# One tile of sources for each block of 128 slots, and four sums in PSUM instead of two pairs of two

## The chip, the cores and the metric

The kernel runs on one core of a Trainium2 chip. The metric is the device time of one execution, in microseconds (us), from the start to the end of the program; a lower time is better. A core has five engines that run their own queues of instructions: TensorE (PE, with its weight loads as PEld), VectorE (DVE), ScalarE (ACT), GpSimd (POOL) and SyncE (SP). Each engine has a sequencer that reads its queue in order, does the register and semaphore instructions itself and hands the others to the engine; the profile marks what the sequencer does with a q (DVEq, PEldq).

## The reference

Four layers are added in turn to `x`, 2500 nodes by 256 features. The change touches the third, a graph attention with two heads of 128 features over 40000 edges, and the sort of the edges that it needs:

```python
def _gat_head(node_feats, W, a, src, dst, N):
    h = node_feats @ W
    a_l, a_r = (a[0, :C], a[0, C:])
    s_l = h @ a_l
    s_r = h @ a_r
    logits = s_l[src] + s_r[dst]
    e = jnp.exp(-jax.nn.leaky_relu(logits, negative_slope=ALPHA))
    row_sum = jax.ops.segment_sum(e, src, num_segments=N)
    h_prime = jax.ops.segment_sum(e[:, None] * h[dst], src, num_segments=N)
    return jax.nn.elu(h_prime / row_sum[:, None])
...
x = x + _L0_gnn_ref(_layernorm(x, axis=-1), edge_attr_256, src, dst, ...)
x = x + _L0_ffn_ref(_layernorm(x, axis=-1)[None], ...)[0]
x = x + _L1_gnn_ref(_layernorm(x, axis=-1), ..., edge_index, 2500)
x = x + _L1_ffn_ref(_layernorm(x, axis=-1)[None], ...)[0]
```

The first layer is a message passing over the same edges, the second a mixture of 16 experts with the best two of each node, the fourth an attention over 64 slices.

## The kernel before, in words

**Tiles of nodes.** The 2500 nodes stand as 125 lanes by 20 tiles; node n is in lane n // 20 of tile n % 20 (`LANES`, `TILES`).

**The sort.** So that a block of edges adds into one tile of sources, the edges are sorted by the tile of their source. Each tile's edges get a run of slots; the run is padded to a multiple of `unit` slots. Before, `unit` is `PAIR` = 256, so two blocks of 128 slots always share a tile, and the buffers have `PAIR_BLOCKS` = 352 blocks. With these inputs the 20 tiles have 1923 to 2083 edges each. Padded to 256 they fill 326 blocks, the last 26 of the 352 hold no edge at all; padded to 128 they would fill 323. The counting runs during the first layer (`count_bucket`), the numbering of the slots (`BucketSort.number`, L274 to L314) on VectorE at the start of `node_mlp`, before that stage's own work, and the last three instructions of it (L310, L313, L314) find for each pair of blocks its tile: a comparison of every pair's number with the 20 tile ends, on one lane, then a sum. Its result is `tile_row`. The placing of edges into slots (`Placing`, L354 to L381) is spread over the 54 blocks of the mixture of experts: for each of 320 columns of edges VectorE and ScalarE make one-hot rows and TensorE multiplies them twice into a table of 352 columns (L380).

**The attention over edges** (`attend_edges`, L1711 to L1898) works in groups of four blocks (`GROUP` = 4), 88 groups. For a group g

- GpSimd issues four indirect DMAs (L1769), each of which gathers 128 rows of 258 floats (the features and right scores of the edges' other ends) from `head_table` in DRAM into `got`. There are four buffers (`RB` = 4), and GpSimd waits only for the indices, which VectorE copies for group g + 4 in its iteration g (L1836).
- VectorE makes the one-hots of the sources' lanes (L1840), TensorE turns them (L1783), ScalarE copies them out of PSUM (L1820) and widens the others to f32 (L1823), and TensorE multiplies them with the tile's left scores (L1789). VectorE sums the three parts (L1846), adds the right scores once the gather has landed (L1850), applies the leaky relu (L1852), ScalarE the exponential (L1825), and VectorE multiplies the gathered rows by it (L1857, L1860).
- TensorE multiplies one-hots and weighted rows (L1799), two blocks into each of the two sums of `s_ps[u]`; two sets of two sums take turns, and a set is free once the sums of group g - 2 are added.
- VectorE adds each sum to its tile of the accumulator in SBUF (L1868). Which tile it is, it has to read: `tiles_of` (L1738) loads one register from `tile_row` for each sum, and TensorE's queue does the same for the left scores.

The order on VectorE is written out by hand. Iteration g is: one-hots of g + 1, weighting of g (L1857, L1860), indices of g + 4, `tiles_of` and the additions of g - 1, then L1846, L1850 and L1852 of g + 1. On TensorE it is `source_scores(g + 1)` and then `scatter(g)`. Four groups are one turn of a hardware loop.

```python
def accumulate(g, u, first=False):
    tiles = tiles_of(dve, g)
    dve.wait_ge(scattered, g + 1)
    for n, tile in enumerate(tiles):
        if not first or n > 0:
            dve.wait_ge(added, g * UN + n)
        dve.tensor_tensor(acc[:, tile, :], s_ps[u][0:LANES, n, 0:ROW], acc[:, tile, :], ALU.add).then_inc(added, 1)
```

Of the kernel before, what the change touches and what calls it, by code (L numbers as in the profile page):

```python
# [16 lines left out]
P = 128  # L17
# [11 lines left out]

PAIR = 2 * P  # L30
PAIR_BLOCKS = -(-((N_EDGES + TILES * (PAIR - 1)) // PAIR * 2) // (2 * GROUP)) * 2 * GROUP
MOE_BLOCKS = -(-((N_NODES * TOP + EXPERTS * (P - 1)) // P) // 6) * 6
# [78 lines left out]
class Shared:  # L111


    def __init__(self, nc, sb, sem):
# [12 lines left out]
        self.ones = sb("ones", [P, P])  # L127
        self.count_i = sb("count_i", [P, PAIR_BLOCKS], I32)
        self.count = sb("count", [P, PAIR_BLOCKS])
        self.count16 = sb("count16", [P, PAIR_BLOCKS], F16)  # L130
        self.ident16 = sb("ident16", [P, P], BF16)
# [28 lines left out]
def constants(nc, m, io):  # L160

    made = m.constants_made
    with nc.Block() as block:
# [16 lines left out]
        def _(pool):  # L180
# [13 lines left out]
            chain.link(pool.memset(m.ones[:], 1.0))  # L194
            chain.link(pool.iota(m.count_i[:], pattern=[[1, PAIR_BLOCKS]], base=0, channel_multiplier=0))
            chain.link(pool.iota(m.lane_i[:], pattern=[[0, 1]], base=0, channel_multiplier=1))
# [12 lines left out]
class BucketSort:  # L209
# [64 lines left out]
    def number(self, dve):  # L274
# [13 lines left out]
        if self.by_bucket:  # L288
# [8 lines left out]
            chain.link(nc.vector.tensor_tensor(slot[:], slot[:], self.part[:], ALU.add))  # L297
            self.past = seen[0:1].rearrange("p b c -> p (b c)")[:, 0:units * buckets].rearrange("p (u b) -> p u b", b=buckets)
        else:
# [9 lines left out]

        chain.link(nc.vector.tensor_tensor(  # L310
            self.past, m.count[0:1, 0:units].unsqueeze(2).to_broadcast([1, units, buckets]),
            last[0:1, :].unsqueeze(1).to_broadcast([1, units, buckets]), ALU.is_ge))
        chain.link(nc.vector.tensor_reduce(self.tile_f[:], self.past, AX_X, ALU.add))  # L313
        chain.link(nc.vector.tensor_scalar(out.tile_row, self.tile_f[:], float(buckets - 1), None, ALU.min))  # L314
# [1396 lines left out]
def attend_edges(nc, sem, m, r, sl, acc):  # L1711
# [19 lines left out]
    G = GROUP  # L1731
    UN = G * P // PAIR
    groups = PAIR_BLOCKS // G
    turns = groups // RB
# [5 lines left out]
    with ExitStack() as ctx:  # L1740
# [17 lines left out]
        sl_ps = ps("sl_ps", [P, 512])  # L1758
        s_ps = [ps(f"s_ps{u}", [P, UN, 512]) for u in range(2)]
        with nc.Block() as block:  # L1760
# [16 lines left out]
            def _(pe):  # L1777
# [15 lines left out]
                def scatter(g, u, wait_added=True):  # L1793
                    pe.wait_ge(hot_ready, g + 1)
                    pe.wait_ge(scaled, g + 1)
                    if wait_added:
                        pe.wait_ge(added, (g - 1) * UN)
                    for j in range(G):
                        last = nc.tensor.matmul(s_ps[u][0:LANES, j * UN // G, 0:ROW], hot[u][:, j, :], w[u][:, j, :],  # L1799
                                                start=j % (G // UN) == 0, stop=j % (G // UN) == G // UN - 1)  # L1800
                    last.then_inc(scattered, 1)

                source_scores(0, 0)
                for v in range(RB):
                    source_scores(v + 1, (v + 1) % 2)
                    scatter(v, v % 2, v >= 2)
                with pe.Fori(1, turns - 1) as i:
# [8 lines left out]
            @block.scalar  # L1816
            def _(act):
                def one_group(g, u, begun=True):
                    act.wait_ge(turned, g + 1)
                    nc.scalar.activation(hot_t[u][:], t_ps[0:LANES, :, :], ACT.Copy).then_inc(turned_in, 1)  # L1820
                    if begun:
                        act.wait_ge(scattered, g - 1)
                    nc.scalar.activation(hot[u][:], hot16[u][:], ACT.Copy).then_inc(hot_ready, 1)  # L1823
                    act.wait_ge(lrelu_ready, g + 1)
                    nc.scalar.activation(e[u][:], lrelu[u][:], ACT.Exp, scale=-1.0).then_inc(e_ready, 1)  # L1825

                for v in range(RB):
                    one_group(v, v % 2, v >= 2)
                with act.Fori(1, turns) as i:
                    for v in range(RB):  # L1830
                        one_group(RB * i + v, v % 2)

            @block.vector
            def _(dve):
# [27 lines left out]
                def accumulate(g, u, first=False):  # L1862
                    tiles = tiles_of(dve, g)
                    dve.wait_ge(scattered, g + 1)
                    for n, tile in enumerate(tiles):
                        if not first or n > 0:
                            dve.wait_ge(added, g * UN + n)
                        dve.tensor_tensor(acc[:, tile, :], s_ps[u][0:LANES, n, 0:ROW], acc[:, tile, :], ALU.add).then_inc(added, 1)  # L1868

# [578 lines left out]
def gnn_moe_gat_slice_kernel(nc, io_gine, io_moe, io_gat, io_slice, out):  # L2448

    with ExitStack() as ctx:  # L2450
# [3 lines left out]
        def sem(n):  # L2454
            return ctx.enter_context(nc.semaphore(n))

        m = Shared(nc, sb, sem)
        by_src = Ends(sb("slots_by_src_other", [P, PAIR_BLOCKS], I32)[:], sb("slots_by_src_lane", [P, PAIR_BLOCKS])[:],
                      sb("slots_by_src_tile_row", [1, PAIR_BLOCKS // 2], I32)[:])
        constants(nc, m, io_gine)  # L2460
        with ExitStack() as sorting:
            s = EdgeSort(nc, sorting, "by_src", by_src, PAIR_BLOCKS, PAIR)
            gather_and_update(nc, m, io_gine, s)
# [40 lines left out]
```

## Time and profile before

| | |
|---|---|
| three runs | 2787.79, 2793.99 (median), 2800.44 us |
| the profiled execution | 2793.28 us, its span 2791.5 us |
| mean granted clock of TensorE | 0.857 of full speed |
| busy share of the span | PE 75%, PEld 65%, DVE 59%, ACT 36%, POOL 51% |
| L1769, gathers of the attention | 352, 404.5 us busy, 1149 ns each in the mean |
| L1799, TensorE's sums | 704, 276.8 us busy, 561 ns each in the mean |

The profiled execution took 0.7 us less than the median of the runs. The span runs from its first to its last instruction. Times in the rows are us from the start of the span; those of one instruction are its start and its duration. "Idle before" names what ended the time in which the engine had nothing to run; "issue" is time for which the profile shows no wait.

### The profile page before, as it was taken

How to read it: one execution, taken by the hardware profiler on the slowest of the kernel's cores; microseconds unless marked ns; L12 is line 12 of the kernel's file. 1: busy time of each engine (PE TensorE's matmuls, PEld its weight loads, DVE VectorE, ACT ScalarE, POOL GpSimd, SP SyncE). 2: the span in 40 equal slices, each digit the busy share in tenths (PEclk: the TensorE clock that was granted, in tenths of full speed). 3: DMA queues.
4: the chain of work that ended last, by engine and by line, in shares of the span. 5: the costliest groups of instructions: out<-in, count | busy, mean ns of one | idle time of the engine just before them, and what ended most of it. 6: DMA issues, size and time to landing. Idle time of an engine off the chain costs nothing. (4 is left out here: it accounts for less than half of the span.)

```text
span 2791.5 us, 46568 instructions
## 1 busy us (share of the span) xinstructions
PE 2090.2 (75%) x13095; PEld 1806.7 (65%) x13096; DVE 1650.7 (59%) x4813; ACT 1008.1 (36%) x1931; POOL 1409.8 (51%) x1131
## 2 busy tenths in 40 slices
PE   3599989999999999919349999951366766662966
PEld 2588878888888888819338888851344444441855
DVE  5477776766666666666264444444555555556962
ACT  1244444544544444414115555530122222221311
POOL 1487787877877777720001111125377777770000
PEclk9799999999999999969569999985677667675978
DMA  6566666666666666550037677742233333361000
GB/s 166 137 122 132 128 126 131 133 132 129 133 130 132 131 132 128 113 115 1 38 106 236 237 240 245 245 139 57 70 90 89 90 88 92 90 86 31 1 9 37
DMA packets 186354, 325.62 MB, mean 117 GB/s; under 512 B 30014, under 2 KB 111723, under 8 KB 185298
## 3 DMA queue, kind: packets, MB, share of 16 engines
q0 software_dynamic: 85280, 141.65, 25.5%
q1 hardware_dynamic: 100118, 181.83, 21.0%
q10 hardware_dynamic: 900, 1.50, 0.2%
q8 instruction: 24, 0.39, 0.1%
q14 instruction: 32, 0.26, 0.0%
HBM read 260.52 MB, written 64.30 MB: 116 GB/s over the span
## 5 line engine op out<-in xcount | busy, mean ns | idle before, releaser
L631 POOL DMA_INDIRECT edge_sums<-edge_agg,edge_slot x316 | 553.9, 1753 | 174.8 <-issue 78.0
L1769 POOL DMA_INDIRECT att_got<-head_table,att_idx x352 | 404.5, 1149 | 143.7 <-issue 107.0
L622 POOL DMA_INDIRECT edge_nf<-node_table,edge_node_idx x316 | 325.7, 1031 | 152.4 <-issue 88.1
L750 ACT ACTIVATE edge_whole<-edge_h_ps,edge_b 128x512 f32<-128x512 f32 x316 | 216.5, 685 | 480.5 <-PE edge_h_ps L467 477.0
L465 PE MATMUL edge_e_ps<-edge_w_high,edge_hid_low 128*128 128x256 f32 x1264 | 356.7, 282 | 0.1
L466 PE MATMUL edge_e_ps<-edge_w_low,edge_hid_high 128*128 128x256 f32 x1264 | 355.8, 282 | 0.0
L467 PE MATMUL edge_e_ps<-edge_w_high,edge_hid_high 128*128 128x256 f32 x1264 | 355.4, 281 | 0.0
L1799 PE MATMUL att_s_ps<-att_w,att_hot 128*125 128x258 f32 x704 | 276.8, 561 | 4.6 <-issue 3.5
L465 PE MATMUL edge_h_ps<-edge_eat_high,edge_w_low 128*128 128x512 f32 x632 | 248.9, 394 | 23.6 <-DVE edge_eat_low L810 23.6
L1361 POOL DMA_INDIRECT moe_rows<-node_table,moe_idx x54 | 51.7, 958 | 398.4 <-DVE moe_idx L1472 398.1
L467 PE MATMUL edge_h_ps<-edge_eat_high,edge_w_high 128*128 128x512 f32 x632 | 252.3, 399 | 0.0
L819 DVE TENSOR_TENSOR edge_hid_low<-edge_whole,edge_hid_high 128x512 fp32r<-128x512 f32 x316 | 218.9, 693 | 54.3 <-ACT edge_hid_high L755 48.6
L466 PE MATMUL edge_h_ps<-edge_eat_low,edge_w_high 128*128 128x512 f32 x632 | 249.7, 395 | 0.0
L824 DVE TENSOR_TENSOR edge_pre<-edge_e_ps,edge_nf 128x1024 f32<-128x1024 f32 x79 | 96.8, 1225 | 257.6 <-DMA edge_nf<-node_table,edge_node_idx 205.2
L465 PEld LDWEIGHTS edge_e_ps<-edge_w_high,edge_hid_low 128*128 128x128 f32 x1264 | 244.6, 194 | 0.3 <-DVE edge_hid_low L819 0.3
L466 PEld LDWEIGHTS edge_e_ps<-edge_w_low,edge_hid_high 128*128 128x128 f32 x1264 | 244.3, 193 | 0.0
L467 PEld LDWEIGHTS edge_e_ps<-edge_w_high,edge_hid_high 128*128 128x128 f32 x1264 | 243.8, 193 | 0.0
L1799 PEld LDWEIGHTS att_s_ps<-att_w,att_hot 128*125 128x125 f32 x704 | 185.1, 276 | 47.2 <-issue 4.4
L1411 PE MATMUL moe_h_ps<-moe_xt,moe_w 128*128 128x128 f32 x1728 | 206.2, 278 | 10.7 <-DMA moe_w<-in_L_ffn_w_dram 8.9
L1411 PEld LDWEIGHTS moe_h_ps<-moe_xt,moe_w 128*128 128x128 f32 x1728 | 199.1, 193 | 17.2 <-issue 8.5
L1783 PEld LDWEIGHTS att_t_ps<-ident,att_hot 128*125 128x125 bf16 x352 | 38.0, 177 | 185.2 <-DVE att_hot L1840 180.3
L1783 PE MATMUL att_t_ps<-ident,att_hot 128*125 128x128 bf16 x352 | 48.2, 275 | 139.6 <-DVE att_hot L1840 139.1
(344 smaller groups left out, 4526.5 us busy)
## 6 DMA issues: line engine op xcount, KB each, us to landing
moe_w<-in_L_ffn_w_dram SPq DMA_DIRECT2D x162, 512.0 KB, 4.7
edge_ea<-in_edge_attr_dram SPq DMA_DIRECT2D x77, 448.0 KB, 5.1
edge_dst_row<-dst_rows SPq DMA_DIRECT2D x79, 256.0 KB, 4.5
routed<-moe_out SPq DMA_DIRECT2D x54, 128.0 KB, 6.2
att_got<-head_table,att_idx POOLq DMA_INDIRECT x352, 2.8
edge_nf<-node_table,edge_node_idx POOLq DMA_INDIRECT x316
edge_sums<-edge_agg,edge_slot POOLq DMA_INDIRECT x316
edge_ea<-in_edge_attr_dram SPq DMA_DIRECT2D x77, 64.0 KB, 5.4
```

The source lines that it names most:

```text
L465: pe.matmul(out, ll, rh, start=start, stop=False)
L466: pe.matmul(out, lh, rl, start=False, stop=False)
L467: return pe.matmul(out, lh, rh, start=False, stop=stop)
L622: pool.indirect_dma_start(nf[u][:, j, :], None, m.node_table[:, :], bass.IndirectOffsetOnAxis(ap=node_idx[u][:, j:j + 1], axis=0)).then_in ...
L631: pool.indirect_dma_start(m.sums[k][:, :], bass.IndirectOffsetOnAxis(ap=slot[u][:, j:j + 1], axis=0), agg[u][:, j, :], None, compute_op=AL ...
L750: act.activation(whole[c][:], h_ps[:, c % 2, 0:N], ACT.Relu, bias=b1[:, c:c + 1]).then_inc(hid_whole, 1)
L819: nc.vector.tensor_tensor(hidl[:, c, :], whole[c][:], hidh[:, c, :].bitcast(F32), ALU.subtract).then_inc(hid_ready, 1)
L824: nc.vector.tensor_tensor(pre[:], e_ps[:], nf[u][:], ALU.add).then_inc(summed, 1)
L1411: last = nc.tensor.matmul(h_ps[:, c, :], w[:, kd, c * P:(c + 1) * P], xt[u][:, kd, :], start=kd == 0, stop=kd == KD - 1)
L1769: pool.indirect_dma_start(got[v][:, j, :], None, m.head_table[:, :], bass.IndirectOffsetOnAxis(ap=idx[v][:, j:j + 1], axis=0)).then_inc(la ...
L1783: last = nc.tensor.transpose(t_ps[0:LANES, j, :], hot16[u][:, j, :], m.ident16[:])
L1799: last = nc.tensor.matmul(s_ps[u][0:LANES, j * UN // G, 0:ROW], hot[u][:, j, :], w[u][:, j, :], start=j % (G // UN) == 0, stop=j % (G // U ...
```

## The change

The unit of the sort becomes 128 slots, so each block has a tile of its own; `SRC_BLOCKS` is 336, in 84 groups. `tile_row` has 336 entries instead of 176. The comparison for it no longer fits its buffer at once and is done in two halves of 168 by 20. `s_ps` is one set of four sums: block j of every group has sum j, TensorE waits before each matmul for the addition of sum j of the group before, and VectorE waits before each addition for its own matmul. `UN`, the number of sums and of register loads in a group, goes from 2 to 4. A matmul no longer adds to the one before it in PSUM.

```diff
--- before.py
+++ after.py
@@ -27,8 +27,7 @@
 GROUP = 4
 
 
-PAIR = 2 * P
-PAIR_BLOCKS = -(-((N_EDGES + TILES * (PAIR - 1)) // PAIR * 2) // (2 * GROUP)) * 2 * GROUP
+SRC_BLOCKS = -(-((N_EDGES + TILES * (P - 1)) // P) // (4 * GROUP)) * 4 * GROUP
 MOE_BLOCKS = -(-((N_NODES * TOP + EXPERTS * (P - 1)) // P) // 6) * 6
 NODE_MID = N_NODES // 2
 SUMS = 2
...
@@ -295,7 +294,7 @@
                 chain.link(last_slots)
                 chain.link(nc.vector.tensor_reduce(to[:], self.numbers[:].rearrange("p b c -> p c b"), AX_X, ALU.add))
             chain.link(nc.vector.tensor_tensor(slot[:], slot[:], self.part[:], ALU.add))
-            self.past = seen[0:1].rearrange("p b c -> p (b c)")[:, 0:units * buckets].rearrange("p (u b) -> p u b", b=buckets)
+            self.past = seen[0:1].rearrange("p b c -> p (b c)")[:, 0:units // 2 * buckets].rearrange("p (u b) -> p u b", b=buckets)
         else:
             for b in range(buckets):
                 last_slots = nc.vector.scalar_tensor_tensor(seen[:, b, :], seen[:, b, :], off[:, b:b + 1], mask[:, b, :], ALU.add, ALU.mult)
@@ -307,10 +306,12 @@
         chain.link(nc.vector.tensor_scalar(slot_i[:], slot_i[:], P - 1, None, ALU.bitwise_and))
         chain.link(nc.vector.tensor_copy(out.pos, slot_i[:]))
 
-        chain.link(nc.vector.tensor_tensor(
-            self.past, m.count[0:1, 0:units].unsqueeze(2).to_broadcast([1, units, buckets]),
-            last[0:1, :].unsqueeze(1).to_broadcast([1, units, buckets]), ALU.is_ge))
-        chain.link(nc.vector.tensor_reduce(self.tile_f[:], self.past, AX_X, ALU.add))
+        some = self.past.shape[1]
+        for a in range(0, units, some):
+            chain.link(nc.vector.tensor_tensor(
+                self.past, m.count[0:1, a:a + some].unsqueeze(2).to_broadcast([1, some, buckets]),
+                last[0:1, :].unsqueeze(1).to_broadcast([1, some, buckets]), ALU.is_ge))
+            chain.link(nc.vector.tensor_reduce(self.tile_f[:, a:a + some], self.past, AX_X, ALU.add))
         chain.link(nc.vector.tensor_scalar(out.tile_row, self.tile_f[:], float(buckets - 1), None, ALU.min))
 
 
@@ -1729,8 +1730,8 @@
     scattered = sem("att_scattered")
     added = sem("att_added")
     G = GROUP
-    UN = G * P // PAIR
-    groups = PAIR_BLOCKS // G
+    UN = G
+    groups = SRC_BLOCKS // G
     turns = groups // RB
     assert groups % RB == 0
 
@@ -1756,7 +1757,7 @@
         w = sb("w", [P, G, ROW])
         t_ps = ctx.enter_context(nc.psum_tensor("att_t_ps", [P, G, P], BF16))
         sl_ps = ps("sl_ps", [P, 512])
-        s_ps = [ps(f"s_ps{u}", [P, UN, 512]) for u in range(2)]
+        s_ps = ps("s_ps", [P, UN, 512])
         with nc.Block() as block:
 
             @block.gpsimd
@@ -1793,17 +1794,15 @@
                 def scatter(g, u, wait_added=True):
                     pe.wait_ge(hot_ready, g + 1)
                     pe.wait_ge(scaled, g + 1)
-                    if wait_added:
-                        pe.wait_ge(added, (g - 1) * UN)
                     for j in range(G):
-                        last = nc.tensor.matmul(s_ps[u][0:LANES, j * UN // G, 0:ROW], hot[u][:, j, :], w[u][:, j, :],
-                                                start=j % (G // UN) == 0, stop=j % (G // UN) == G // UN - 1)
-                    last.then_inc(scattered, 1)
+                        if wait_added:
+                            pe.wait_ge(added, g * UN + (j - UN + 1))
+                        nc.tensor.matmul(s_ps[0:LANES, j, 0:ROW], hot[u][:, j, :], w[u][:, j, :], start=True, stop=True).then_inc(scattered, 1)
 
                 source_scores(0, 0)
                 for v in range(RB):
                     source_scores(v + 1, (v + 1) % 2)
-                    scatter(v, v % 2, v >= 2)
+                    scatter(v, v % 2, v >= 1)
                 with pe.Fori(1, turns - 1) as i:
                     for v in range(RB):
                         source_scores(RB * i + (v + 1), (v + 1) % 2)
@@ -1819,7 +1818,7 @@
                     act.wait_ge(turned, g + 1)
                     nc.scalar.activation(hot_t[u][:], t_ps[0:LANES, :, :], ACT.Copy).then_inc(turned_in, 1)
                     if begun:
-                        act.wait_ge(scattered, g - 1)
+                        act.wait_ge(scattered, (g - 1) * UN)
                     nc.scalar.activation(hot[u][:], hot16[u][:], ACT.Copy).then_inc(hot_ready, 1)
                     act.wait_ge(lrelu_ready, g + 1)
                     nc.scalar.activation(e[u][:], lrelu[u][:], ACT.Exp, scale=-1.0).then_inc(e_ready, 1)
@@ -1861,11 +1860,11 @@
 
                 def accumulate(g, u, first=False):
                     tiles = tiles_of(dve, g)
-                    dve.wait_ge(scattered, g + 1)
                     for n, tile in enumerate(tiles):
+                        dve.wait_ge(scattered, g * UN + (n + 1))
                         if not first or n > 0:
                             dve.wait_ge(added, g * UN + n)
-                        dve.tensor_tensor(acc[:, tile, :], s_ps[u][0:LANES, n, 0:ROW], acc[:, tile, :], ALU.add).then_inc(added, 1)
+                        dve.tensor_tensor(acc[:, tile, :], s_ps[0:LANES, n, 0:ROW], acc[:, tile, :], ALU.add).then_inc(added, 1)
 
                 def one_group(g, v, first=False, start=False):
                     u = v % 2
@@ -2455,11 +2454,11 @@
             return ctx.enter_context(nc.semaphore(n))
 
         m = Shared(nc, sb, sem)
-        by_src = Ends(sb("slots_by_src_other", [P, PAIR_BLOCKS], I32)[:], sb("slots_by_src_lane", [P, PAIR_BLOCKS])[:],
-                      sb("slots_by_src_tile_row", [1, PAIR_BLOCKS // 2], I32)[:])
+        by_src = Ends(sb("slots_by_src_other", [P, SRC_BLOCKS], I32)[:], sb("slots_by_src_lane", [P, SRC_BLOCKS])[:],
+                      sb("slots_by_src_tile_row", [1, SRC_BLOCKS], I32)[:])
         constants(nc, m, io_gine)
         with ExitStack() as sorting:
-            s = EdgeSort(nc, sorting, "by_src", by_src, PAIR_BLOCKS, PAIR)
+            s = EdgeSort(nc, sorting, "by_src", by_src, SRC_BLOCKS, P)
             gather_and_update(nc, m, io_gine, s)
             mixture(nc, sem, m, io_moe, s)
         graph_attention(nc, sem, m, io_gat, by_src)
```

## Rows read from the trace of the kernel before

**Rows 1.** The page: busy tenths of 40 slices of the span

```profile
POOL 1487787877877777720001111125377777770000
```

**Rows 2.** Waits from 2006 to 2528 us: us in total, times, longest

```profile
DVE att_z L1850 <- DMA att_got<-head_table,att_idx: 183.6, 85, 3.8
...
POOL att_got L1769 <- issue: 105.5, 346, 0.3
```

**Rows 3.** Timeline of GpSimd in the middle of the attention: start us, us

```profile
2204.98 2.14 POOL L1769 DMA_INDIRECT att_got<-head_table,att_idx  x1 [0.30 <-issue]
2207.42 0.95 POOL L1769 DMA_INDIRECT att_got<-head_table,att_idx  x1 [0.30 <-issue]
```

**Rows 4.** Timeline of VectorE, one group between two landings: start us, us

```profile
2204.08 0.17 DVE L1850 TENSOR_TENSOR att_z<-att_parts,att_got 128x8 f32<-128x8 f32 x1 [2.45 <-DMA att_got<-head_table,att_idx]
...
2205.06 1.22 DVE L1857 TENSOR_TENSOR att_w<-att_got,att_e 128x1024 f32<-128x1024 f32 x1
...
2206.65 1.00 DVE L1868 TENSOR_TENSOR gat_acc<-att_s_ps,gat_acc 125x258 f32 x2 [0.21 <-issue]
...
2207.56 0.17 DVE L1846 TENSOR_REDUCE att_parts<-att_sl_ps 128x8 f32<-128x24 f32 x1
...
2210.33 0.17 DVE L1850 TENSOR_TENSOR att_z<-att_parts,att_got 128x8 f32<-128x8 f32 x1 [2.60 <-DMA att_got<-head_table,att_idx]
...
2212.89 0.43 DVE L1868 TENSOR_TENSOR gat_acc<-att_s_ps,gat_acc 125x258 f32 x1 [0.22 <-issue]
```

**Rows 5.** Instructions of L1738, 2205.0 to 2206.6 us: duration ns min/median/max, first and last start

```profile
L1738 DVEq TENSOR_LOAD <-slots_by_src_tile_row x2: 300/301/302, 2205.1 to 2205.8; - x2
L1738 DVEq SEQ_ASSERT  x2: 23/23/23, 2205.7 to 2206.4; - x2
```

**Rows 6.** Timeline of VectorE, a group at the loop's turn

```profile
2240.29 0.17 DVE L1850 TENSOR_TENSOR att_z<-att_parts,att_got 128x8 f32<-128x8 f32 x1 [2.57 <-DMA att_got<-head_table,att_idx]
...
2243.38 1.00 DVE L1868 TENSOR_TENSOR gat_acc<-att_s_ps,gat_acc 125x258 f32 x2 [0.18 <-issue]
```

**Rows 7.** Timeline of VectorE, an L1850 that waits for nothing

```profile
2315.95 0.17 DVE L1846 TENSOR_REDUCE att_parts<-att_sl_ps 128x8 f32<-128x24 f32 x1
2316.26 0.17 DVE L1850 TENSOR_TENSOR att_z<-att_parts,att_got 128x8 f32<-128x8 f32 x1
```

**Rows 8.** TensorE: loads of L1738 from 2206 us, and its timeline

```profile
L1738 PEldq TENSOR_LOAD <-slots_by_src_tile_row x2: 299/304/310, 2206.8 to 2207.6; - x2
...
2201.24 3.80 PE L1799 MATMUL att_s_ps<-att_w,att_hot 128*125 128x258 f32 x8
...
2205.20 0.44 PE L1783 MATMUL att_t_ps<-ident,att_hot 128*125 128x128 bf16 x4 [0.17 <-DVE att_hot L1840]
...
2206.42 0.33 PE L1789 MATMUL att_sl_ps<-gat_sl_parts,att_hot_t 125*128 x4 [0.77 <-ACT att_hot_t L1820]
```

**Rows 9.** Timeline of VectorE: start and end of the attention

```profile
2006.14 0.17 DVE L1850 TENSOR_TENSOR att_z<-att_parts,att_got 128x8 f32<-128x8 f32 x1
...
2016.14 0.17 DVE L1850 TENSOR_TENSOR att_z<-att_parts,att_got 128x8 f32<-128x8 f32 x1 [1.66 <-DMA att_got<-head_table,att_idx]
...
2521.22 0.17 DVE L1850 TENSOR_TENSOR att_z<-att_parts,att_got 128x8 f32<-128x8 f32 x1 [2.79 <-DMA att_got<-head_table,att_idx]
...
2527.20 1.00 DVE L1868 TENSOR_TENSOR gat_acc<-att_s_ps,gat_acc 125x258 f32 x2 [2.87 <-PE att_s_ps L1799]
```

**Rows 10.** The two wide instructions of the sort's end

```profile
L310 DVE TENSOR_TENSOR spare_rows<-count,by_src_sort_last x1: 3811/3811/3811, 1245.6 to 1245.6; 1x3520 f16<-1x3520 f32 x1
...
L313 DVE TENSOR_REDUCE by_src_sort_tile_f<-spare_rows x1: 3807/3807/3807, 1249.4 to 1249.4; 1x176 f32<-1x3520 f16 x1
```

**Rows 11.** Groups by line, 1600 to 1800 us: us busy, mean ns

```profile
L380 PE MATMUL by_src_place_tables<-by_src_place_which,by_src_place_rows 125*128 125x352 f16 x324 | 52.8, 312 | 0.0
```

**Rows 12.** Blocks without edges: L1850 before them, and a window among them

```profile
2474.58 0.17 DVE L1850 TENSOR_TENSOR att_z<-att_parts,att_got 128x8 f32<-128x8 f32 x1 [2.41 <-DMA att_got<-head_table,att_idx]
...
2480.00:2490.00 10.00, 5.63 (x23) 3.33 (x22) 4.64 (x19) 1.52 (x4) 7.82 (x8) 0.75 0.92 78
```

More of the change, by code:

```diff
@@ L127, in __init__ @@
         self.ones = sb("ones", [P, P])
-        self.count_i = sb("count_i", [P, PAIR_BLOCKS], I32)
-        self.count = sb("count", [P, PAIR_BLOCKS])
-        self.count16 = sb("count16", [P, PAIR_BLOCKS], F16)
+        self.count_i = sb("count_i", [P, SRC_BLOCKS], I32)
+        self.count = sb("count", [P, SRC_BLOCKS])
+        self.count16 = sb("count16", [P, SRC_BLOCKS], F16)
         self.ident16 = sb("ident16", [P, P], BF16)
@@ L194, in _ @@
             chain.link(pool.memset(m.ones[:], 1.0))
-            chain.link(pool.iota(m.count_i[:], pattern=[[1, PAIR_BLOCKS]], base=0, channel_multiplier=0))
+            chain.link(pool.iota(m.count_i[:], pattern=[[1, SRC_BLOCKS]], base=0, channel_multiplier=0))
             chain.link(pool.iota(m.lane_i[:], pattern=[[0, 1]], base=0, channel_multiplier=1))
```

## Prediction

> **What bounds the attention now.** I read the 40 slices of the page first: in the slices of the attention GpSimd is busy seven tenths of the time [rows 1]. It doesn't look full. The waits settle it: VectorE waits 183.6 us, 85 times, for a gather to land, 2.16 us in each group, while GpSimd's idle time is 0.30 us between any two gathers and nothing else [rows 2]. So the issue of gathers sets the pace, and VectorE has about 2 us to spare in a group.
>
> A gather takes 0.95 us and 0.30 us follow, 1.256 us a block, 5.02 us a group. But a gather that starts within 0.1 us of L1857 on VectorE takes 2.14 us [rows 3, 4]: it is held for the 1.22 us of that multiplication. From the first L1850 to the last are 515.08 us, 87 groups [rows 9], 5.92 us each; the excess over 5.02 is this hold, and at the end something else: the blocks without edges, which all gather one row, keep the DMA engines 92% busy in the window shown [rows 12], and there the landings are 6.6 us apart ((2521.22 - 2474.58) / 7).
>
> What VectorE needs on its own, waiting for no gather, comes from the timeline. From L1850 to the first addition are 2.57 us (2206.65 - 2204.08), from there to L1846 0.91 us [rows 4], and from L1846 to the next L1850, where that waits for nothing, 0.31 us [rows 7]: 3.79 us. In one group of four, at the turn of the loop, the first part is 3.09 us [rows 6]: 4.31 us. The mean is 3.92 us.
>
> **What sets the first addition.** Two register loads stand ahead of it. They begin at 2205.1 and 2205.8 us, 0.70 us apart, since each has arithmetic and a check behind it; the second check is at 2206.4 us [rows 5], and the addition starts at 2206.65 us with 0.21 us of "issue" before it [rows 4]. The loads thus run beside L1857 and outlast it and the small copies behind it by those 0.2 us. Their cover is used up: any further load delays the addition by all of its 0.70 us. That is the centre of this prediction.
>
> **The change, part by part.**
>
> *Two more loads in VectorE's queue.* 2 x 0.70 = +1.40 us in a group.
>
> *Two more additions.* The two now take 1.00 us from the start of the first to the end of the second, and one is 0.43 us [rows 4], so the second starts 0.57 us after the first. 2 x 0.57 = +1.15 us. Their waits for the matmuls cost nothing: the scatter of g - 1 was done a group earlier.
>
> VectorE's own group becomes 3.79 + 2.55 = 6.34 us, at the turn 6.86 us, in the mean 6.47 us. That is over the 5.92 us which gathers need now. VectorE becomes the bound, by 0.55 us a group, and the gathers run ahead until all four buffers are full; then they start after L1836, when L1857 is over, so the hold goes away too, but off the path. The slow blocks at the end are hidden by the same lead of three groups.
>
> The Trainium skill (SBUF — State Buffer, "Who interferes with whom") says that a VectorE instruction with at most one SBUF input, outside the two-port modes, doesn't contend with GpSimd, and infers that one with two SBUF inputs blocks only reads there and not the writing of descriptors. The first agrees with this trace: the gather at 2207.42 us starts while the additions run, whose one input is in PSUM, and takes 0.95 us [rows 3, 4]. The second doesn't: L1857 has both inputs in SBUF and holds a gather by 1.19 us. By the page's second rule gathers would cost 5.02 us a group, by the row 5.92 us; with VectorE at 6.47 us neither enters the sum.
>
> *One set of sums.* TensorE now waits for sum j of g - 1 before block j of g. VectorE makes these additions right behind the weighting of g that TensorE needs anyway. Block 0 can start 0.43 us after the first addition does, 4.4 us after L1850; the next L1857 is a group later. In the slow stretches a scatter takes 3.80 us and ends 8.2 us after L1850; its sums are wanted 6.47 + 3.97 = 10.4 us after it. No wait of VectorE comes of it.
>
> *Two more loads in TensorE's queue.* There they are 0.8 us apart and begin when the scatter has been issued, beside its execution [rows 8]. Four take 3.1 us, from 6.2 us after L1850 (the last sum is free) to 9.3 us. The transposes, ScalarE's copy and the scores take 1.55 us (2205.20 to 2206.75) [rows 8], to 10.9 us. They are wanted by L1846 of the next group at 6.47 + 6.0 = 12.5 us. Covered, with 1.6 us to spare; this is the cover that matters if the loads are slower than I think.
>
> *The sum for the attention.* The third L1850 is at 2016.1 us now; in the first groups TensorE's added loads have less cover, I take 0.4 us: 2016.5. From there to the 84th are 81 groups, 20 of them at a turn: 61 x 6.34 + 20 x 6.86 = 523.9 us. The first and last four groups are written out with fixed addresses, which saves arithmetic behind a load; I take 2 us for them all, an estimate. The last L1850 is at 2538.4 us against 2521.22. From there to the end of the last addition are 7.0 us now (2528.2 - 2521.2) [rows 9]; then four more loads, 0.6 to 0.7 us each and not beside anything, less what the waiting for TensorE covered, and two more additions: about 10. End of the additions 2548.4 against 2528.2: **+20.2 us**. 16 gathers fewer give nothing back, being off the path.
>
> *The sort's end.* The comparison and the sum are 3.81 us each for 3520 elements on one lane [rows 10]. Now each is done twice for 3360 elements: 4 x 3.64 = 14.6 us instead of 7.6: **+7.0 us**. VectorE's chain is what `node_mlp` begins with, and nothing covers it: its first products wait for weights that are split behind it.
>
> *The placing.* The table has 16 columns fewer. 324 matmuls of 352 columns hold TensorE for 52.8 us in 200 us [rows 11], 163 ns each; 16/352 of that is 7.4 ns, times 640 is 4.7 us. TensorE is the bound there but for a few waits on weights; between 0 and 4.7 I take **-4 us**. The narrower comparisons on VectorE are covered.
>
> Together +23 us on the profiled 2793.28 us: 2816.5, and the median of the runs is 0.7 us above the profiled execution: **2817 us**. Each 0.1 us by which VectorE's group differs from 6.47 us is 8 us.
>
> **Rivals.**
>
> *A. The gathers stay the bound, and the kernel is faster.* If two added loads ran further beside L1857, or cost VectorE less than 0.35 us each, a group would need under 5.9 us. Then the last L1850 comes earlier by the groups saved. All slots with edges are in groups 0 to 80, as those of before in 0 to 81; then three groups at 6.6 us follow instead of six: with the mixed one, 2521.2 - 26. With the sort and the placing that is 2793 - 26 + 1 + 7 - 4 = 2771 us. For it: VectorE has 2 us to spare, and two additions alone, 1.15 us, fit in. Against it: the loads run one after the other and already outlast their cover. It decides at an addition of 2.0 us to VectorE's group; break-even for the whole time is at 2.26 us.
>
> *B. The same, with the hold gone.* If the addition is 1.3 to 1.6 us, VectorE is just late enough that L1857 falls between two gathers: 5.3 us a group, some 47 us less than A, 2725 us. It needs loads that cost 0.1 to 0.2 us; the rows speak against it.
>
> *C. TensorE becomes part of the ring.* The waits for single sums tie its queue to VectorE's, and if the four loads don't run beside the scatter (276.8 us of L1799 in 88 groups, 3.15 us each), a group is 3.1 + 1.55 + 3.15 = 7.8 us: 1.3 us more, 108 us, 2925 us. It decides once more than 1.8 us of the scatter is not beside the loads (6.47 - 4.65). Against it: the loads start at 2206.8 us, right after the scores end (2206.75), so when the scatter that is queued ahead of them has hardly begun [rows 8].
>
> **How the numbers follow.** 0.67 for the forecast, 0.15 for A, 0.03 for B, 0.06 for C, and 0.09 for loads partly covered, where the gain and the loss about cancel (2785 to 2800). The forecast's own range is 2802 to 2832, from +-0.15 us a group and the bounds of the placing. To hold 8 in 10 it goes to 2788 below and 2845 above. A measurement tells some 0.5%, 14 us, from no change: faster is under 2780, slower over 2808. From A, B: 0.18 faster; the partly covered case and the lower edge of the forecast: 0.18 same; 0.64 slower.
>
> **What would show it.** Right: VectorE's waits for landings all but gone after the first fifteen groups or so; GpSimd waiting for L1836's indices instead; L1850s about 6.34 us apart; the first addition some 4 us after L1850 with over 1 us of "issue" before it; no gathers of 2.1 us in the middle; two pairs at L310 and L313 of 3.6 us each. Wrong: "issue" before the additions still 0.2 us, or VectorE still waiting for gathers (A, B), or L1846 waiting for TensorE in most groups (C).

## The result, and the profile after

The changed kernel takes 2834.5 us (median of 4 runs, 2833.2 to 2837.6) against 2794.4 us: 1.0155 of the time before, 95% interval 1.0134 to 1.0176, so 40 us or 1.3 to 1.8% slower. Slower was forecast, at 2817 us; the measured time is inside the range of 2788 to 2845. The profiled execution took 2834.7 us, its span is 2833.0 us, 41.5 us above that of before.

The page's slices again, GpSimd's and VectorE's, against [rows 1]:

```profile
DVE  5577776666666666666254444446466666667863
...
POOL 1477887777777777720001111143465556550000
```

In the attention GpSimd is now busy four to six tenths of the time instead of seven. The waits of the attention (us in total, times, longest) say why, against [rows 2]:

```profile
DVE gat_acc L1867 <- issue: 126.3, 80, 1.7
POOL att_got L1770 <- DVE att_idx L1835: 120.1, 64, 2.2
...
DVE gat_acc L1867 <- DVE gat_acc L1867: 53.2, 239, 0.6
...
DVE gat_acc L1867 <- PE att_s_ps L1800: 8.2, 17, 2.3
```

VectorE no longer waits for any landing. GpSimd waits 120.1 us for indices that VectorE copies. And VectorE stands idle for 126.3 us with nothing to wait for, ahead of its additions, where before it was 0.2 us a group. TensorE's granted clock in the attention, a mean over full and half speed, is lower too, 0.63 instead of 0.70; but VectorE waits only 8.2 us for TensorE's sums, so that isn't what slows it. One group on VectorE (start us, us), against [rows 4]:

```profile
2207.54 0.17 DVE L1849 TENSOR_TENSOR att_z<-att_parts,att_got 128x8 f32<-128x8 f32 x1
...
2208.52 1.22 DVE L1856 TENSOR_TENSOR att_w<-att_got,att_e 128x1024 f32<-128x1024 f32 x1
...
2209.73 0.16 DVE L1835 COPY att_idx<-slots_by_src_other 128x4 int32 x1
...
2211.53 0.43 DVE L1867 TENSOR_TENSOR gat_acc<-att_s_ps,gat_acc 125x258 f32 x1 [1.64 <-issue]
...
2212.17 0.43 DVE L1867 TENSOR_TENSOR gat_acc<-att_s_ps,gat_acc 125x258 f32 x1 [0.21 <-DVE gat_acc L1867]
...
2212.80 0.43 DVE L1867 TENSOR_TENSOR gat_acc<-att_s_ps,gat_acc 125x258 f32 x1 [0.21 <-DVE gat_acc L1867]
...
2213.44 0.43 DVE L1867 TENSOR_TENSOR gat_acc<-att_s_ps,gat_acc 125x258 f32 x1 [0.21 <-DVE gat_acc L1867]
2213.79 0.17 DVE L1845 TENSOR_REDUCE att_parts<-att_sl_ps 128x8 f32<-128x24 f32 x1
2213.99 0.17 DVE L1849 TENSOR_TENSOR att_z<-att_parts,att_got 128x8 f32<-128x8 f32 x1
```

From L1849 (which was L1850) to the first addition are 3.99 us, where it was 2.57. The weighting and the copies are over at 2209.89 us; 1.64 us of nothing follow. In that time the queue does this (duration ns min/median/max, first and last start), against [rows 5]:

```profile
L1739 PEldq TENSOR_LOAD <-slots_by_src_tile_row x4: 298/298/311, 2207.5 to 2209.7; - x4
...
L1739 DVEq TENSOR_LOAD <-slots_by_src_tile_row x4: 299/300/310, 2208.6 to 2210.7; - x4
```

Four loads of VectorE, at 2208.6 to 2210.7 us, 0.70 us apart; the last ends with its arithmetic at 2211.3. The turn of the loop costs what it did, some 0.5 us: in the group before this one L1849 is at 2200.49 us and the first addition at 2204.97, 4.48 us later [rows 6].

The whole attention: the first and last L1849, the two halves of the sort's end, and the end of the first layer's edge stage in both kernels:

```profile
L1849 DVE TENSOR_TENSOR att_z<-att_parts,att_got x84: 166/167/229, 2018.9 to 2561.9; 128x8 f32<-128x8 f32 x84
```

```profile
L311 DVE TENSOR_TENSOR spare_rows<-count,by_src_sort_last x2: 3646/3646/3647, 1256.1 to 1263.5; 1x3360 f16<-1x3360 f32 x2
```

```profile
L314 DVE TENSOR_REDUCE by_src_sort_tile_f<-spare_rows x2: 3641/3642/3642, 1259.8 to 1267.1; 1x168 f32<-1x3360 f16 x2
```

```profile
L824 DVE TENSOR_TENSOR edge_pre<-edge_e_ps,edge_nf x79: 1224/1225/1227, 74.1 to 1197.7; 128x1024 f32<-128x1024 f32 x79
```

```profile
L825 DVE TENSOR_TENSOR edge_pre<-edge_e_ps,edge_nf x79: 1224/1225/1227, 75.3 to 1207.5; 128x1024 f32<-128x1024 f32 x79
```

The last L1849 is 543.0 us behind the first, in 83 steps of 6.54 us (before 515.1 in 87 steps of 5.92). The sort's end takes 14.6 us instead of 7.6. And one thing stands here that was not forecast: the edge stage, from the first to the last `edge_pre`, takes 1132.2 us instead of 1123.6, with the same instructions.

So the 41.5 us are: 27.9 between the first and the last L1849, 3.3 behind it, 7.0 in the sort, 8.6 in the edge stage and 2.0 around it, -3.1 in the mixture, and -4.2 in the rest.

### The profile page after: what moved, and what is told of

It is laid out like the page before. It is cut to its first block and busy times, and to the rows that moved or that the text cites. A ratio compares the mean times of both kernels' runs of the same rounds, so it can differ in the third digit from the quotient of the medians.

```text
span 2833.0 us, 48614 instructions
## 1 busy us (share of the span) xinstructions
PE 2134.2 (75%) x13031; PEld 1830.3 (65%) x13032; DVE 1715.7 (61%) x4935; ACT 1002.3 (35%) x1919; POOL 1335.6 (47%) x1115
## 5 line engine op out<-in xcount | busy, mean ns | idle before, releaser
L1770 POOL DMA_INDIRECT att_got<-head_table,att_idx x336 | 327.5, 975 | 244.5 <-DVE att_idx L1835 156.7
L1800 PE MATMUL att_s_ps<-att_w,att_hot 128*125 128x258 f32 x672 | 294.2, 613 | 6.2 <-DVE gat_acc L1867 2.9
L1867 DVE TENSOR_TENSOR gat_acc<-att_s_ps,gat_acc 125x258 f32 x336 | 143.3, 427 | 187.7 <-issue 126.3
L1800 PEld LDWEIGHTS att_s_ps<-att_w,att_hot 128*125 128x125 f32 x672 | 193.0, 303 | 59.4 <-issue 4.2
```

Of the source, the lines that this page charges most:

```text
L1770: pool.indirect_dma_start(got[v][:, j, :], None, m.head_table[:, :], bass.IndirectOffsetOnAxis(ap=idx[v][:, j:j + 1], axis=0)).then_inc(la ...
L1800: nc.tensor.matmul(s_ps[0:LANES, j, 0:ROW], hot[u][:, j, :], w[u][:, j, :], start=True, stop=True).then_inc(scattered, 1)
L1867: dve.tensor_tensor(acc[:, tile, :], s_ps[0:LANES, n, 0:ROW], acc[:, tile, :], ALU.add).then_inc(added, 1)
```

## The experiments

Each of the twelve kernels below the first two rows was timed beside the kernel before on the same chip, and the ratio is to that kernel's time there: 2790.9 us for e1 to e4, 2786.9 us for e5 to e8, 2794.0 us for e9 to e12. "Attention" is the time from the first to the last L1849 or L1850 in the profiled execution.

| kernel | built on | median us | ratio (95%) | attention us | edge stage us |
|---|---|---|---|---|---|
| before | | 2794.4 | | 515.1 | 1123.6 |
| after | | 2834.5 | 1.0155 (1.0134 to 1.0176) | 543.0 | 1132.2 |
| e1_two_loads | after | 2747.0 | 0.9845 (0.9829 to 0.9861) | 453.1 | 1132.3 |
| e2_more_loads | before | 2779.4 | 0.9952 (0.9935 to 0.9969) | 502.4 | 1124.7 |
| e3_spread_loads | after | 2772.3 | 0.9928 (0.9910 to 0.9946) | 480.6 | 1128.7 |
| e4_packed | after | 2744.9 | 0.9831 (0.9814 to 0.9847) | 462.3 | 1133.9 |
| e5_aligned | after | 2831.7 | 1.0156 (1.0115 to 1.0198) | 543.0 | 1127.3 |
| e6_shifted | before | 2797.0 | 1.0033 (1.0011 to 1.0056) | 512.4 | 1125.4 |
| e7_e_in_psum | before | 2724.5 | 0.9772 (0.9733 to 0.9812) | 449.0 | 1125.7 |
| e8_packed_psum | after | 2753.5 | 0.9886 (0.9836 to 0.9936) | 462.9 | 1121.0 |
| e9_one_set | before | 2794.2 | 1.0002 (0.9985 to 1.0019) | 509.6 | 1124.8 |
| e10_pe_two_loads | after | 2835.6 | 1.0134 (1.0113 to 1.0155) | 542.5 | 1131.3 |
| e11_336_in_pairs | before | 2770.0 | 0.9914 (0.9898 to 0.9931) | 483.8 | 1128.3 |
| e12_336_e_in_psum | before | 2701.2 | 0.9670 (0.9650 to 0.9689) | 423.1 | 1133.4 |

### Is it VectorE's loads? (e1, e10)

Theory 1 is the prediction's: the loads in VectorE's queue set the pace. Theory 2 is rival C: TensorE and the single set of sums make a ring.

```diff
 def accumulate(g, u, first=False):
-    tiles = tiles_of(dve, g)
+    some = [dve.value_load(r.tile_row[0:1, bass.DynSlice(g * UN + n, 1)], min_val=0, max_val=TILES - 1) for n in (0, 2)]
+    tiles = [some[0], some[0], some[1], some[1]]
```

> The changed kernel, but VectorE loads two registers in a group instead of four and uses each for two additions (so some blocks are added to the wrong tile; the work is the same). TensorE still loads four, and the one set of sums stays. Theory 1 (the loads in VectorE's queue, 0.70 us each, set the pace): VectorE's group falls from 6.54 to about 5.1 us; the gathers bound it again, at 5.2 to 5.9 us depending on how often L1856 holds them; 83 groups give 54 to 111 us back: 2724 to 2780 us. Theory 2 (TensorE's four loads and the one set of sums make a ring that sets the pace): unchanged, 2830 to 2838 us.

The other takes the same two loads out of TensorE's queue:

```diff
 def source_scores(g, u):
-    tiles = tiles_of(pe, g)
+    some = [pe.value_load(r.tile_row[0:1, bass.DynSlice(g * UN + n, 1)], min_val=0, max_val=TILES - 1) for n in (0, 2)]
+    tiles = [some[0], some[0], some[1], some[1]]
```

> The changed kernel, but TensorE loads two registers in a group instead of four and uses each for two blocks (so some blocks read the scores of the wrong tile); VectorE loads four as before. Theory 1: TensorE's loads run beside its scatter and nothing changes, 2830 to 2837 us. Theory 2: as much comes back as with two loads on VectorE, 2747 us.

Two loads less on VectorE give 88 us (2834.5 to 2747.0), the same on TensorE nothing (2835.6). The timeline of VectorE in e1, one group:

```profile
2204.69 0.17 DVE L1849 TENSOR_TENSOR att_z<-att_parts,att_got 128x8 f32<-128x8 f32 x1
...
2207.23 0.96 DVE L1868 TENSOR_TENSOR gat_acc<-att_s_ps,gat_acc 125x258 f32 x2 [0.17 <-issue]
2208.41 0.96 DVE L1868 TENSOR_TENSOR gat_acc<-att_s_ps,gat_acc 125x258 f32 x2 [0.22 <-DVE gat_acc L1868]
...
2209.91 0.17 DVE L1849 TENSOR_TENSOR att_z<-att_parts,att_got 128x8 f32<-128x8 f32 x1
```

The first addition comes 2.54 us after L1849, as before the change (2.57), and the group takes 5.22 us with all four additions in it. GpSimd, which in the changed kernel waited 120.1 us for indices, waits for none:

```profile
POOL att_got L1770 <- issue: 100.5, 330, 0.3
```

So the gathers set the pace again in e1, and the 88 us are less than the two loads took on VectorE (1.4 us in each of 84 groups). What TensorE does with the time it gains in e10 stands in its waits:

```profile
PE att_s_ps L1801 <- DVE gat_acc L1868: 103.2, 82, 2.7
```

It waits 103.2 us for VectorE's additions (2.9 in the changed kernel): earlier in its place, it finds the sums not free. The single set does tie the two queues, but TensorE is the one that waits.

### The loads alone, on the kernel before (e2)

```diff
 def accumulate(g, u, first=False):
+    tiles_of(dve, g)
     tiles = tiles_of(dve, g)
```

> The kernel before with two more register loads in VectorE's queue ahead of the two additions, their values unused. Theory 1: VectorE's own group goes from 3.92 to 5.3 us, below the 5.9 us of the gathers: not slower than 2794 us. If the delay moves L1857 into the gap between two gathers, the hold of 0.9 us a group goes away as well and a group takes 5.3 us: down to 2745 us. A theory in which a load costs its time wherever it stands: 88 x 1.4 = 123 us, 2917 us.

176 loads more, 123 us in VectorE's queue, make the kernel 0.5% faster. VectorE had the time: its waits for landings fall from 183.6 us [rows 2] to

```profile
DVE gat_acc L1869 <- issue: 128.5, 87, 2.3
...
DVE att_z L1850 <- DMA att_got<-head_table,att_idx: 63.3, 40, 2.5
```

and the 128.5 us of "issue" take their place. What is gained is a part of the hold (the gathers between 2040 and 2440 us take 1129 ns in the mean instead of 1173 before); the full slip into the gap, 2745 us, didn't come.

### Loads beside the additions, and one load for four tiles (e3, e4)

```diff
-    tiles = tiles_of(dve, g)
-    for n, tile in enumerate(tiles):
+    tiles = tiles_of(dve, g, (0, 1))
+    for n in range(UN):
...
+        if n + 2 < UN:
+            tiles += tiles_of(dve, g, (n + 2,))
```

> The changed kernel with two of VectorE's four loads moved behind additions 0 and 1, so that they run beside them. Theory 1: the first addition comes 2.6 us after L1849 instead of 4.0, the later two are 0.85 us behind the one before instead of 0.64: a group of 5.6 us (6.1 at the turn), 5.7 in the mean, 0.8 less than now: 83 x 0.8 = 66 us, 2768 us. Theory 2 (TensorE's ring): unchanged.

```diff
+    four = self.tile_f[:].rearrange("p (g j) -> p g j", j=4)
+    chain.link(nc.vector.scalar_tensor_tensor(four[:, :, 0], four[:, :, 1], 32.0, four[:, :, 0], ALU.mult, ALU.add))
+    chain.link(nc.vector.scalar_tensor_tensor(four[:, :, 2], four[:, :, 3], 32.0, four[:, :, 2], ALU.mult, ALU.add))
+    chain.link(nc.vector.scalar_tensor_tensor(out.tile_row, four[:, :, 2], 1024.0, four[:, :, 0], ALU.mult, ALU.add))
...
 def tiles_of(eng, g):
-    return [eng.value_load(r.tile_row[0:1, bass.DynSlice(g * UN + n, 1)], min_val=0, max_val=TILES - 1) for n in range(UN)]
+    four = eng.value_load(r.tile_row[0:1, bass.DynSlice(g, 1)], min_val=0, max_val=32 ** UN - 1)
+    return [((four >> (5 * n)) & 31).with_bounds(min_val=0, max_val=TILES - 1) for n in range(UN)]
```

> The changed kernel with the four tiles of a group packed into one integer at the end of the sort, so that VectorE and TensorE load one register in a group and take the four out by shifts. Theory 1: one load of 0.70 us stays covered by L1856, the first addition comes 2.5 us after L1849, a group of VectorE is 5.0 to 5.4 us; the gathers bound it at 5.2 to 5.9 us: 2724 to 2780 us. If the shifts cost as much as a load, nothing is gained: 2834 us.

Both do the whole of the change's work and undo its loss: 2772.3 us (2768 expected) and 2744.9 us (2724 to 2780 expected), 0.7% and 1.7% faster than before. VectorE's timeline in e3, then in e4:

```profile
2207.55 0.43 DVE L1867 TENSOR_TENSOR gat_acc<-att_s_ps,gat_acc 125x258 f32 x1 [0.25 <-PE att_s_ps L1800]
2208.47 0.43 DVE L1867 TENSOR_TENSOR gat_acc<-att_s_ps,gat_acc 125x258 f32 x1 [0.49 <-DVE gat_acc L1867]
2209.39 0.43 DVE L1867 TENSOR_TENSOR gat_acc<-att_s_ps,gat_acc 125x258 f32 x1 [0.49 <-DVE gat_acc L1867]
2210.03 0.43 DVE L1867 TENSOR_TENSOR gat_acc<-att_s_ps,gat_acc 125x258 f32 x1 [0.21 <-DVE gat_acc L1867]
```

```profile
2203.07 0.17 DVE L1857 TENSOR_TENSOR att_z<-att_parts,att_got 128x8 f32<-128x8 f32 x1
...
2205.34 0.41 DVE L1875 TENSOR_TENSOR gat_acc<-att_s_ps,gat_acc 125x258 f32 x1
...
2206.12 0.43 DVE L1875 TENSOR_TENSOR gat_acc<-att_s_ps,gat_acc 125x258 f32 x1 [0.36 <-DVE gat_acc L1875]
...
2206.91 0.43 DVE L1875 TENSOR_TENSOR gat_acc<-att_s_ps,gat_acc 125x258 f32 x1 [0.36 <-DVE gat_acc L1875]
...
2207.70 0.43 DVE L1875 TENSOR_TENSOR gat_acc<-att_s_ps,gat_acc 125x258 f32 x1 [0.36 <-PE att_s_ps L1808]
...
2208.25 0.17 DVE L1857 TENSOR_TENSOR att_z<-att_parts,att_got 128x8 f32<-128x8 f32 x1
```

In e3 an addition with a load behind it is followed by the next after 0.92 us, and without one after 0.64. In e4 the first addition starts right behind the copies, 2.27 us after L1857 (e4's number for L1849), and the next ones follow 0.79 us apart, since the shifts stand between them. A group is 5.18 us here and 5.57 in the mean; VectorE is still the bound, since it waits for no landing in the attention. The expectation for e3 counted VectorE's instructions alone. But GpSimd has only 0.30 us between any two gathers in e3, and its gathers of 1133 ns in the mean, 78 of the 336 longer than 1.5 us, make 5.75 us a group, about as long as a group takes (5.79). So e3 shows what spreading the loads gives in time, not that VectorE alone sets its pace.

### The single set of sums alone (e9)

```diff
-s_ps = [ps(f"s_ps{u}", [P, UN, 512]) for u in range(2)]
+s_ps = ps("s_ps", [P, UN, 512])
...
-    if wait_added:
-        pe.wait_ge(added, (g - 1) * UN)
     for j in range(G):
+        if wait_added and j % (G // UN) == 0:
+            pe.wait_ge(added, (g - 1) * UN + (j * UN // G + 1))
```

> The kernel before (pairs of blocks, 352 blocks) with one set of two sums in PSUM instead of two sets; TensorE waits before each pair for the addition of the same sum of the group before. This is the change's PSUM part alone. Theory 1: TensorE starts a scatter some 0.5 us later and VectorE wants it a group later, so nothing changes: 2781 to 2795 us. Theory 2 (the single set ties TensorE and VectorE together): L1850 comes later in each group, 20 us or more.

1.0002 (0.9985 to 1.0019): it costs nothing here, where VectorE has 2 us to spare in a group; for the changed kernel it is the waits of e10 and of the result that say so. TensorE waits for the additions, us in total and times, and VectorE as little as before for TensorE:

```profile
PE att_s_ps L1799 <- DVE gat_acc L1868: 24.9, 59, 3.5
...
DVE gat_acc L1868 <- PE att_s_ps L1799: 4.6, 4, 3.0
```

### What the blocks are worth (e11)

```diff
-PAIR_BLOCKS = -(-((N_EDGES + TILES * (PAIR - 1)) // PAIR * 2) // (2 * GROUP)) * 2 * GROUP
+PAIR_BLOCKS = 336
```

> The kernel before with PAIR_BLOCKS set to 336: pairs and all else as before, 16 blocks without edges fewer (these inputs need 326; other inputs could need 352). It gives what the change gives in blocks, at none of its price. The four groups that go are at the slow end, 6.6 us each, and the placing has 16 columns fewer: 26 + 4 us, 2757 us. If the blocks without edges were hidden, only the placing remains: 2783 us.

With the pairs kept, 16 blocks fewer give 24 us (0.9914), 13 us less than expected (2757 us). That is what the change bought and then didn't get: with VectorE as the bound the gathers are off the path. In the profile the attention is 31.3 us shorter, more than the 26 expected, and the edge stage 4.7 us longer.

### The hold (e7, e8, e12)

```diff
-e = sb("e", [P, G, HEADS])
+e = [ps(f"e_ps{u}", [P, 512])[:, 0:G * HEADS].rearrange("p (j h) -> p j h", h=HEADS) for u in range(2)]
```

> The kernel before with the exponentials e written to PSUM (two free banks) instead of SBUF, so that L1857 has one input in SBUF and one in PSUM, as L1868 has. Theory (an instruction of VectorE with both inputs in SBUF holds a gather that starts beside it): no gather of 2.1 us is left, a group takes 5.02 us up to the blocks without edges, 0.86 x 80 = 69 us less: 2725 us. Rival (the gather is held by something else that falls at the same time, as the end of the DMA before): unchanged, 2792 us.

One line, 2724.5 us, 2.3% faster than before (1.9 to 2.7%; 2725 us expected). The multiplication itself is as long as it was, and the longest of 352 gathers is now 1.02 us (instructions of the two lines: count, duration ns min/median/max):

```profile
L1857 DVE TENSOR_TENSOR att_w<-att_got,att_e_ps x88: 1205/1214/1222, 2006.8 to 2455.1; 128x1024 f32<-128x1024 f32 x88
```

```profile
L1769 POOL DMA_INDIRECT att_got<-head_table,att_idx x352: 949/953/1020, 1997.6 to 2439.8; - x176
```

> The changed kernel with packed tiles (as in the run before), the exponentials in PSUM and the buffers back on their multiples of 64. Theory: gathers 5.02 us a group, VectorE 5.1 to 5.4 us: 5.3 us instead of 5.57; with the edge stage 8 us shorter 2715 us. If VectorE's own group was the bound with packed tiles already: 2737 us.

> The same 336 blocks in pairs, with the exponentials in PSUM as well. If the two gains are independent (62 us for the exponentials in PSUM, 30 us for the blocks): 2695 us. With gathers at 5.02 us a group the queue of slow gathers at the end is as long, so most of the second gain should stay; if it is hidden, 2720 us.

In e8 the hold is gone too (the longest gather takes 1.01 us), but the attention is as long as in e4, 462.9 us against 462.3: VectorE was the bound already, which is the mechanism of the second case expected. The time of that case, 2737 us, was missed by 16 us, though the edge stage was short in the profile (1121.0 us). The four runs lie 21 us apart (2743.6 to 2764.2), for a reason that no row shows, so 2753.5 us is not to be read as slower than e4. e12 is the fastest kernel of all, 2701.2 us; it is one for these inputs, since others can need more than 336 blocks.

### The edge stage (e5, e6)

```diff
+sb("gap", [P, 8])
 self.ident16 = sb("ident16", [P, P], BF16)
```

> The changed kernel with an unused buffer of 32 bytes a partition behind the counting buffers. The change makes the buffers in front 160 bytes smaller, and those of the first layer stand 32 bytes off the multiples of 64 at which they stood relative to before; the gap puts them back. The edge stage of the first layer, whose instructions the change doesn't touch, took 1132 us in the profile of the changed kernel (1123.6 before), and 1129 to 1134 in three kernels built on it (1124.7 in the one built on before). Theory (addresses): the stage falls to 1124 us, the total to 2826. Rival (anything else, as chance from run to run): it stays near 1132.

> The kernel before with the same unused 32 bytes, which shifts all later buffers by 32. Theory (addresses): the edge stage goes from 1124 to 1132 us, the total from 2792 to 2800. Rival: unchanged.

Neither came as expected. Shifting the buffers of the kernel before left the stage at 1125.4 us. Putting those of the changed kernel back gave 1127.3 us, a little over half of the difference, and 2831.7 us in the total, which against the kernel before is the same ratio as without the gap (1.0156). In the table the stage takes 1123.6 to 1125.7 us in the five kernels with counting buffers of 352, 1128.3 to 1133.9 us in the seven with 336, and 1121.0 and 1127.3 us in the two with 336 and the gap. The longer stage comes with the 336 columns also in e11 and e12, whose attention is coded as before, so it isn't the attention's code. That it is where the buffers lie is not shown: e6 moved them and nothing followed, and each of these figures is one execution. TensorE's clock doesn't explain it: its 6832 matmuls of the stage are busy 1034.8 us in the changed kernel and 1026.7 before, but 1029.1 us in e10, where the stage is as long (1131.3). The cause stays open. e6 was 0.3% slower than before as a whole with a stage only 1.8 us longer, so the total doesn't settle it either.

## Why the prediction was right, and what it missed

**The bound moves to VectorE, because the loads had used up their cover.** Right, and shown from three sides: in the profile (no wait for a landing, 126.3 us of "issue" ahead of the additions), by e1 against e10, and by e2. The first addition was forecast 3.97 us after L1849 and is 3.99.

**VectorE's group** was forecast at 6.34 us, 6.86 at the turn; in the loop it is 6.47 and 7.07 in the mean. This is the term that was too small. The prediction priced the new waits of each addition for its own matmul at nothing, since the matmul is long done. The matmul is, but the additions start 0.64 us apart, not 0.57: the second wait has become an instruction of its own,

```profile
L1866 DVEq EVENT_SEMAPHORE  x4: 21/21/21, 2211.4 to 2213.3; - x4
```

four in a group instead of one. Behind it stands the register instruction that the address needs, which was there before. The trace of e1 takes the two apart. Its second addition of a pair uses the address of the first, so it has the wait but not that instruction, which stands there twice for four additions:

```profile
L1868 DVEq FUSED_REGOPS  x2: 64/64/64, 2207.1 to 2208.3; - x2
```

Within a pair the additions start 0.53 us apart, between the pairs 0.64 again. With the wait alone it is thus 0.53, with the register instruction alone 0.57 (before), with both 0.64: the wait costs some 0.07 us. No run took it away alone.

Three distances of 0.07 us, and 0.11 more in every fourth group, would make 18 us over the 76 groups of the loop, more than the 10.5 us by which the groups from the third L1849 (2029.5 us) to the 84th (2561.9) exceed the forecast's 521.9. Some 8 us were forecast too high. The step from L1845 to L1849 was taken as 0.31 us and is 0.21 in half of the groups, as in the one shown, where it gives back half of what the waits cost. The first addition is 3.88 to 3.92 us after L1849 in two groups of four. And the five written-out groups in this stretch take 5.81 us each, 3 us less in all where 2 were taken. So this part of the sum came closer than its terms did.

**Start and tail.** The third L1849 comes 10.5 us after the first (10.4 forecast), the end of the additions 10.3 us after the last (10). The attention as a whole costs 31.2 us where 20.2 were forecast.

**The sort's end:** +7.0 us (7.0). **The placing:** the mixture is 3.1 us shorter (4). **The single set of sums:** nothing, right (e9). **TensorE's loads:** covered, right (e10); rival C falls with it.

**Rivals A and B** fall as forecasts. What they say of the gathers holds once the loads are gone: with two loads (e1) VectorE's group is short enough for the gathers to matter again, and the kernel is 1.6% faster than before, at 2747.0 us between A's 2771 and B's 2725. B's mechanism, that a later VectorE loses less to the hold, showed weakly in e2.

**Not in the forecast:** the edge stage, +8.6 us in the profile. It and the 11 us of the attention make up the difference between +23 forecast and +40 measured; the rest about cancels. Both misses go the same way, and 2834.5 us lies 2.5 us above the forecast's own range of 2802 to 2832. It is the wider range, to 2845, that holds it, and no term of the prediction stood behind that widening. The mechanism was right; that the time falls inside the range is in part luck.

## What to carry to other kernels

A register load with its arithmetic and check takes the queue 0.70 us here, and costs nothing only while the engine has something to run ahead of it; before adding one, look at whether the instruction behind the loads already shows "issue" before it. If it does, load beside the instructions that use the values, or pack several values into one word (0.7 and 1.7% faster here than before the change, instead of 1.6% slower). And where GpSimd's gathers set the pace, look for a long instruction of VectorE with both inputs in SBUF beside them, before saving on gathers.

## What the runs showed of the hardware

- The multiplication with both inputs in SBUF held a gather that started beside it, 2.14 us instead of 0.95; with one input in PSUM, at the same 1.21 us, it held none (longest of 352: 1.02 us). The Trainium skill (SBUF — State Buffer, "Who interferes with whom") says that a VectorE instruction with two SBUF inputs contends with a GpSimd instruction that reads SBUF. The gather is one, since it reads its indices from `att_idx` in SBUF, so the hold agrees with that sentence. The prediction set the hold against the page's other statement, an inference that such an instruction leaves the writing of descriptors alone; no run here separates the reading of the indices from that writing, so the inference is neither shown nor refuted.
- Blocks without edges, all of whose slots gather one row, kept the DMA engines 92% busy [rows 12], and landed 6.6 us apart in groups of four. Ordinary ones took 35%, by a window of the kernel before (the last figures are the granted clock, the DMA share and GB/s):

```profile
2460.00:2470.00 10.00, 7.21 (x32) 5.00 (x32) 5.59 (x22) 2.02 (x5) 7.56 (x9) 0.77 0.35 97
```

- Time put into a queue can pay: 123 us of unused loads on VectorE made the kernel 0.5% faster (e2), with gathers of 1129 ns instead of 1173 in the middle of the attention.
